# Row gathers without a bounds check, and VectorE operands read from PSUM, in a three-layer graph convolution

## What is computed

```python
deg = segment_sum(ones, dst)
norm = rsqrt(deg)[src] * rsqrt(deg)[dst]
def conv(h, W, b):
    xw = h @ W
    return segment_sum(xw[src] * norm[:, None], dst) + b
h = conv(conv(conv(x, W1, b1), W2, b2), W3, b3)
out = layernorm(x + h)          # over the 512 features, eps 1e-5
```

## Time and profile before

| | before |
|---|---|
| median of 3 runs | 3510.13 us (3508.68 to 3517.03) |
| profiled execution, its own time | 3509.13 us |
| its span in the trace | 3507.1 us |
| TensorE granted clock over the span | 0.963 |
| TensorE busy | 2637.4 us (75%) |
| GpSimd busy | 2574.0 us (73%) |
| VectorE busy | 1133.2 us (32%) |
| ScalarE busy | 126.9 us (4%) |

### The profile page before, as it was taken

One profiled execution on the slowest core, in us unless ns is written; L12 is line 12 of the kernel. 1 busy time (PEld: TensorE's weight loads), 2 busy tenths in 40 slices (PEclk: granted clock), 3 DMA queues, 4 the chain that ended last, 5 costly groups with the idle time before them and its releaser, 6 DMA issues.

```text
span 3507.1 us, 23852 instructions
## 1 busy us (share of the span) xinstructions
PE 2637.4 (75%) x6574; PEld 1095.7 (31%) x6574; DVE 1133.2 (32%) x2036; ACT 126.9 (4%) x222; POOL 2574.0 (73%) x2511
## 2 busy tenths in 40 slices
PE   7788888888888867777777777766777777777776
PEld 5233333333333322222222222222222222222222
DVE  7222222222222222222222222232434443443334
ACT  1000000000000000000000000000000000000000
POOL 0677777777777657777777777767777777777775
PEclk9999999999999989999999999998999999999998
DMA  8677777777777657777777777766777777777776
GB/s 292 200 211 208 209 207 207 207 204 207 210 207 206 194 154 212 209 209 210 210 208 206 209 208 206 207 193 194 220 216 222 220 219 220 219 223 218 221 213 180
DMA packets 243792, 736.23 MB, mean 210 GB/s; under 512 B 43286, under 2 KB 44946, under 8 KB 243664
## 3 DMA queue, kind: packets, MB, share of 16 engines
q0 software_dynamic: 199440, 653.68, 65.3%
q1 hardware_dynamic: 44224, 81.08, 6.3%
HBM read 683.39 MB, written 51.20 MB: 209 GB/s over the span
## 4 chain that ended last, share of the span: by engine, by line
POOL 48%; issue 14%; POOLq 1%; PE 1%; DMA 1%; DVE 0%; ACT 0%; DVEq 0%
POOL ring L386 48%; POOLq L386 1%; PE ps L549 1%; DMA y_dram<-acc 0%; DMA ring<-y_dram,src_idx 0%; PE ps L602 0%; DVE acc L879 0%; ACT acc L683 0%; DVEq L876 0%; DVE h_sb L901 0%; DVE ln L907 0%; DVE h_sb L905 0%; POOLq L77 0%; DVE row_sb L887 0%; DVE h_sb L887 0%
## 5 line engine op out<-in xcount | busy, mean ns | idle before, releaser
L386 POOL DMA_INDIRECT ring<-y_dram,src_idx x2493 | 2571.1, 1031 | 910.6 <-issue 758.9
L549 PE MATMUL ps<-ring,onehot 128*128 128x512 f32 x4986 | 2371.7, 622 | 829.3 <-DMA ring<-y_dram,src_idx 757.2
L549 PEld LDWEIGHTS ps<-ring,onehot 128*128 128x128 f32 x4986 | 938.4, 197 | 2226.8 <-issue 1792.8
L879 DVE SCALAR_TENSOR_TENSOR acc<-ps,mask,acc 128x512 f32 x624 | 439.8, 747 | 1291.5 <-PE ps L549 1171.5
L861 DVE TENSOR_TENSOR onehot<-place_iota,lo_f 128x512 f32<-128x512 f32 x624 | 428.8, 688 | 879.5 <-PE ps L549 879.5
L575 PE MATMUL ps<-w,w_sb 128*128 128x512 f32 x376 | 169.0, 592 | 0.0
L683 ACT ACTIVATE acc<-h_sb,dinv 128x512 f32<-128x512 f32 x96 | 69.3, 721 | 1488.8 <-DVE h_sb L887 1488.8
L575 PEld LDWEIGHTS ps<-w,w_sb 128*128 128x128 f32 x376 | 71.4, 190 | 89.9 <-issue 89.9
L887 DVE SCALAR_TENSOR_TENSOR h_sb<-ps,dinv,bias 128x512 f32<-128x512 f32 x48 | 36.0, 751 | 135.2 <-PE ps L575 128.9
L679 ACT ACTIVATE w_sb<-ps 128x512 f32<-128x512 f32 x47 | 28.1, 597 | 667.2 <-PE ps L559 667.2
L687 ACT ACTIVATE ln<-ln 128x1 f32<-128x1 f32 x49 | 9.9, 203 | 1123.2 <-DVE ln L913 1123.2
(11 more groups left out here) (105 smaller groups left out, 164.3 us busy)
## 6 DMA issues: line engine op xcount, KB each, us to landing
ring<-y_dram,src_idx POOLq DMA_INDIRECT x2493, 3.8
y_dram<-acc SPq DMA_DIRECT2D x96, 256.0 KB
acc<-in_x_dram SPq DMA_DIRECT2D x1, 12288.0 KB
y_dram<-acc SPq DMA_DIRECT2D x12, 1024.0 KB
w_sb<-in_x_dram SPq DMA_DIRECT2D x48, 256.0 KB, 4.7
out_dram<-row_sb SPq DMA_DIRECT2D x48, 256.0 KB
w_sb<-in_L_gnn_W_dram SPq DMA_DIRECT2D x1, 1024.0 KB
w<-in_L_gnn_W_dram SPq DMA_DIRECT2D x1, 1024.0 KB
```

The lines of the kernel that those rows point to most:

```text
L386: pool.indirect_dma_start(ring[:, s, :], None, y_dram[layer], bass.IndirectOffsetOnAxis(ap=rows, axis=0), bounds_check=N - 1, oob_is_err=F ...
L549: mm = pe.matmul(ps[:, g % BANKS, :], onehot[:, r, k, :], ring[:, r * CPQ + k, :], start=(opens and k == 0), stop=(closes and k == chunks ...
L879: dve.scalar_tensor_tensor(out=rows, in0=ps[:, g % BANKS, :], scalar=mask[:, part, own:own + 1], in1=rows, op0=ALU.mult, op1=ALU.add).then ...
```

## The change

The indirect DMA is issued without `bounds_check` and `oob_is_err`. ScalarE copies three kinds of operand from SBUF into PSUM, and VectorE reads them there:

- `place_iota` once in the prelude, into 128 columns of bank 7 (`iota_ps`), read by `stage_places`;
- the bias of layer 1, and later that of layer 2, into bank 5, at the start of each of these layers (`spread_bias`);
- the x rows of each tile of layer 2 but the last two into bank 4 (`spread_x`), after their load and after the x step of the tile before.

In `norm_rows` the first instruction now adds the bias and the second adds x. SP's queue now waits for the x copy (`x_spread`) before it loads the next x rows. Since bank 7 is taken, the last two tiles of layer 0 are turned into banks 4 and 6 in place of 6 and 7.

```diff
-        LAST_TURN_BANK, LAST_PRODUCT_BANK = 6, 2
+        LAST_TURN_BANKS, LAST_PRODUCT_BANK = (4, 6), 2
+        X_BANK, BIAS_BANK, IOTA_BANK = 4, 5, 7
+        iota_ps = ps[:, IOTA_BANK, 2 * P:3 * P]
...
             def load_and_finish(t):
                 if not is_static(t, 0):
-                    sp.wait_ge(ln_step, LN_STEPS * t + (1 - LN_STEPS))
+                    sp.wait_ge(x_spread, t)
...
                 pool.indirect_dma_start(ring[:, s, :], None, y_dram[layer],
-                                        bass.IndirectOffsetOnAxis(ap=rows, axis=0),
-                                        bounds_check=N - 1, oob_is_err=False).then_inc(done, 16)
+                                        bass.IndirectOffsetOnAxis(ap=rows, axis=0)).then_inc(done, 16)
...
-                        mm = pe.transpose(ps[:, LAST_TURN_BANK + j, k * P:(k + 1) * P], rows[:, k * P:(k + 1) * P], ident[:, :])
+                        mm = pe.transpose(ps[:, LAST_TURN_BANKS[j], k * P:(k + 1) * P], rows[:, k * P:(k + 1) * P], ident[:, :])
...
         def _(act):
+            act.wait_ge(consts_ready, CONSTS)
+            act.copy(iota_ps, place_iota[:, :]).then_inc(iota_spread, 1)
             act.wait_ge(edges_turned, 1)
...
+            def spread_bias(layer):
+                if layer > 0:
+                    act.copy(ps[:, BIAS_BANK, :], bias[:, layer, :]).then_inc(bias_spread, 1)
+
+            def spread_x(t):
+                act.wait_ge(x_loaded, 16 * t + 16)
+                if not is_static(t, 0):
+                    act.wait_ge(ln_step, LN_STEPS * t + (2 - LN_STEPS))
+                act.copy(ps[:, X_BANK, :], x_sb).then_inc(x_spread, 1)
...
             def fast_tile(layer, t):
...
                 else:
+                    spread_x(t)
                     std(t)
...
                 for layer in range(LAYERS):
+                    spread_bias(layer)
                     for t in range(LOOP_TILES):
                         fast_tile(layer, t)
...
-                dve.tensor_tensor(onehot[:, n % RING_QUADS, :, :], place_iota[:, :].unsqueeze(1).broadcast_to([P, CPQ, P]),
+                dve.tensor_tensor(onehot[:, n % RING_QUADS, :, :], iota_ps.unsqueeze(1).broadcast_to([P, CPQ, P]),
...
-                                         scalar=dinv[:, bass.ds(t, 1)], in1=bias[:, layer, :],
+                                         scalar=dinv[:, bass.ds(t, 1)], in1=bias[:, 0, :] if layer == 0 else ps[:, BIAS_BANK, :],
...
+                dve.scalar_tensor_tensor(out=row, in0=tile_of(t), scalar=dinv[:, bass.ds(t, 1)], in1=ps[:, BIAS_BANK, :],
+                                         op0=ALU.mult, op1=ALU.add).then_inc(ln_step, 1)
                 if last is None:
-                    dve.wait_ge(x_loaded, 16 * t + 16)
+                    dve.wait_ge(x_spread, t + 1)
...
-                dve.scalar_tensor_tensor(out=row, in0=tile_of(t), scalar=dinv[:, bass.ds(t, 1)],
-                                         in1=x_sb if last is None else last_x[last],
-                                         op0=ALU.mult, op1=ALU.add).then_inc(ln_step, 1)
                 dve.wait_ge(ln_step, done + 1)
-                dve.tensor_tensor(row, row, bias[:, LAYERS - 1, :], ALU.add).then_inc(ln_step, 1)
+                dve.tensor_tensor(row, row, ps[:, X_BANK, :] if last is None else last_x[last], ALU.add).then_inc(ln_step, 1)
...
                     dve.wait_ge(y_ready, TILES * layer)
+                    dve.wait_ge(bias_spread, layer)
...
+                dve.wait_ge(iota_spread, 1)
                 for n in range(EARLY_QUADS):
```

More of the change, by code:

```diff
@@ L178, in gcn_three_layers_resnorm @@
         ORDER_BANK, TURN_BANK, PRODUCT_BANK, DEG_BANK = 4, 4, 5, 7
-        LAST_TURN_BANK, LAST_PRODUCT_BANK = 6, 2
+        LAST_TURN_BANKS, LAST_PRODUCT_BANK = (4, 6), 2
+        X_BANK, BIAS_BANK, IOTA_BANK = 4, 5, 7
         GROUP_BANK = 4
+        iota_ps = ps[:, IOTA_BANK, 2 * P:3 * P]
         turned = ps[:, :, :].rearrange("p b n -> p (b n)")
         consts_ready = sem("consts_ready")
+        iota_spread = sem("iota_spread")
+        bias_spread = sem("bias_spread")
+        x_spread = sem("x_spread")
         pads_ready = sem("pads_ready")
@@ L710, in last_tiles @@
                         act.wait_ge(tile_turned, LOOP_TILES + k + 1)
-                        act.activation(last_turned[k], ps[:, LAST_TURN_BANK + k, :], ACT.Copy).then_inc(turn_copied, 1)
+                        act.activation(last_turned[k], ps[:, LAST_TURN_BANKS[k], :], ACT.Copy).then_inc(turn_copied, 1)
                 for k in range(2):
```

## The result

The changed kernel takes 3293.45 us (3293.05 to 3295.0, 4 runs), the kernel before 3510.9 us beside it. The ratio is 0.9379, with a 95% interval of 0.9363 to 0.9395: 217 us less, where 87 us less were forecast. The time lies in the range; the gain is two and a half times the forecast one.

A forecast was written before the change was run, and what follows sets the result against it. GpSimd's chain of 2493 gathers was taken to bound the kernel. From the median 3510.1 us, 83.1 us for moved operands and 3.6 us for the check came off, giving 3423.4 us, range 3282 to 3450.

The forecast's parts named there:

- The bound: GpSimd's chain sets the span: first gather at 106.0, gathers 2571.1, idle between them 808.3, tail 21.7, together 3507.1 us.
- Part 1: Iota, bias and x read from PSUM: gathers no longer held up by VectorE instructions with two SBUF tensors, -83.1 us.
- Part 2: Gathers without the bounds check: taken as one more column of a GpSimd instruction, 1.45 ns each, -3.6 us in all.
- The serial bound: Check inside the gather walking over the 128 rows one after the other at 1.45 ns: 185 ns each, 461 us.
- The first rival: The check inside each gather costs more, between 5 and 98 ns: 3415 down to 3183 us, 2966 if serial; chance 0.30.
- The MOVE: The check's instruction in GpSimd's queue, 0.03 us in the gap between gathers: free, the gap stays 0.30 us.
- Parts 3 to 6: VectorE's PSUM operands, ScalarE's copies, layer 2's x chain and the exchanged banks: nothing added to the forecast time.
- part 3: VectorE instructions with a PSUM operand: some 6 ns slower each, 5 us on an engine that waits, nothing in the tail.
- part 5: Layer 2's x load, ScalarE copy, then VectorE: 11.5 us left, 3.6 us for the one early tile; cost 0.
- PSUM without effect: Rival: one-hots hold up the gather wherever their iota lies, so only the check's 3.6 us are gained: 3506.5 us; chance 0.05.
- a late x: Rival: layer 2's x copy misses its 11.5 us and VectorE's additions stall 0.5 us in 47 tiles: 3447 us; chance 0.03.
- a dearer unchecked gather: Rival: the gather without the check takes another, dearer path in its code; at 98 ns more, 3671 us; chance 0.05.

## Why the prediction came out as it did

**The bound: right.** The span was read as a sum on GpSimd, and after the change the same four terms sum to it again.

**Part 1, the moved operands: right in mechanism and size.** Forecast -83.1 us. With the check kept, the gathers went from 2571.1 to 2490.2 us, -80.9; the missing 2.2 us are in 28 gathers that were held up under the last scaling of a tile, 3.3 us together (see the last section). This third cause the prediction didn't have: it said that no gather would be above some 1010 ns, and the longest are 1199 ns there and 1116 ns in the changed kernel. Nor did it have that the operands are worth more without the check: 92.7 us (2450.5 to 2357.8), because more gathers then began under a one-hot. Of the rule in the Trainium skill ("SBUF — State Buffer", Who interferes with whom), the part on two SBUF inputs agrees with all four kernels whose one-hots read SBUF, by 0.21 to 0.24 us for each gather that begins under one, and with the four that read PSUM, by less than 0.002 us. From the same section the prediction took the inference that such an instruction would not hold up a DMA. For these indirect DMAs the measurement differs, and decides. Whether what waits is the gather's read of its index list or something else in it, no run shows.

**Part 2, the bounds check: the step that failed.** Of the three bounds I took "one more column of a GpSimd instruction", 1.45 ns and 3.6 us in all; it measured 52 ns and 129.6 us. The reasoning that led there was "the index list has one column, so it is nearest to the first row". That compares the shape of the operand; what the chip showed is a price that hardly depends on the rows, 42 ns at 32 and at 64 of them. The nearer row was the one that I put at the other end, the shortest whole instruction with 98 ns, almost all of it fixed. The serial bound (185 ns) is out as well, and with it my remark in the rivals that 7.8 ns a row speaks for work row by row: 128 rows against 32 are 81 ns. The first rival, "the check is dear", is the case that happened, at 0.30; its span of 3183 to 3415 us holds the time, and the range reached to it.

**The MOVE: right.** The gap was 0.30 us with and without it. Reading the end of the queue, where MOVEs had run out, gave the answer ahead of time.

**Parts 3 to 6: nothing on the path, as forecast, with a wrong sign in part 3 and a thin margin in part 5.** VectorE's instructions with a PSUM operand are not slower but 3 to 8 ns faster (685 against 688, 737 against 745), so the sign of part 3 was wrong and its size nothing. Among x copies the early tile came closest: its copy began at 3261.52 us, and the x addition at 3262.98 us, right behind the step before it:

```profile
3257.04 0.43 SPq L331 DMA_DIRECT2D w_sb<-in_x_dram  x1
3261.52 0.59 ACT L699 COPY ps<-w_sb 128x512 f32<-128x512 f32 x1 [5.68 <-DMA w_sb<-in_x_dram]
3262.13 0.75 DVE L917 SCALAR_TENSOR_TENSOR h_sb<-acc,dinv,ps 128x512 f32<-128x512 f32 x1 [2.67 <-PE ps L553]
3262.98 0.69 DVE L924 TENSOR_TENSOR h_sb<-h_sb,ps 128x512 f32<-128x512 f32 x1
```

That leaves 0.9 us. The prediction had 3.6 us from the rows of before, and one instruction (some 0.8 us) on top. The margin shrank because the tile's first step now came 5.1 us after the load was issued (3257.04 to 3262.13), against 8.9 us in the earlier trace rows. The copy ended 0.02 us ahead of that first step, so with the x addition first it would just have been in time as well; no run tried that order. Every other tile had over 9 us.

**The other rivals.** PSUM without effect, a late x and a dearer unchecked gather are each out by the rows above.

## What to carry to other kernels

Where one short instruction repeated thousands of times sets the pace, take its minimum, median and maximum first. The spread tells what others do to it (here VectorE instructions with two SBUF tensors), and can be priced from the trace; an option of the instruction itself hides in the minimum, which no trace without that option can price. Give such an option a wide share of the range, or measure it alone. Here the gather was mostly fixed cost (865 of 946 ns at a quarter of the rows) and so was the option; that another option behaves so is a guess. And a gain on the pacing engine shows only where it does set the pace: the kernel with the check as an error was 1.5% faster than the kernel before on one chip, and not faster (3787.79 against 3783.91 us) on the one where the engines waited for something else and TensorE's mean clock was 0.878.

## What the runs showed that was not expected

**A gather of 32 rows costs 865 ns, one of 128 rows 946.** From 32 to 128, rows are nearly free; what counts is the number of instructions.

**The scaling of a finished tile and a gather hold each other up, in either order.** In the kernel before, 38 of its 49 instances began 0.49 to 0.50 us after a gather began and took 0.72 to 0.74 us; the others took 0.55. Start plus lengthening comes to 0.68 us into the gather. Without the check it comes to 0.65 us, from five starts between 0.44 and 0.62 us (iota from SBUF) and 33 between 0.54 and 0.55 us (check taken off). So the gather holds the scaling up to that moment, and not to its own end at 0.95 or 1.00 us. A gather and the lengthened scaling that began under it, then one of the short ones, from the timeline of the kernel before:

```profile
3448.42 1.00 POOL L386 DMA_INDIRECT ring<-y_dram,src_idx  x1 [0.30 <-issue]
...
3448.92 0.73 DVE L919 TENSOR_SCALAR row_sb<-h_sb,ln 128x512 f32<-128x512 f32 x1
```

```profile
3469.98 0.55 DVE L919 TENSOR_SCALAR row_sb<-h_sb,ln 128x512 f32<-128x512 f32 x1
```

That they began at the same point of a gather I put down to the two instructions of the same tile with two SBUF tensors (bias and x additions): they hold up the gather ahead, and so bring the two engines into step. No run tests this by itself, but the runs fit it. With bias and x in SBUF the starts fall together without the check too (33 of 49 within 0.01 us when only the check is off; 32 of 49 in two clusters hardly wider with the iota in PSUM). With every operand in PSUM they don't: with the check put back most are spread from 0.71 to 1.09 us, and in the changed kernel they are spread over the gather, and the group's mean fell from 690 to 551 ns (with it the 33.1 us of VectorE's time to 26.4). In the other order the gather waits, as in the timeline of the changed kernel:

```profile
3056.50 0.55 DVE L938 TENSOR_SCALAR row_sb<-h_sb,ln 128x512 f32<-128x512 f32 x1
```

```profile
3056.76 1.12 POOL L391 DMA_INDIRECT ring<-y_dram,src_idx  x1 [0.30 <-issue]
```

This instruction has one SBUF input; the Trainium skill (the same section) names VectorE's two-port modes as a second cause. The trace fits this, 512 columns in 0.55 us against 0.69 for the two-tensor form, but it doesn't record the mode. The prediction gave the rule without this exception. Gathers held up by this instruction are most of what is left of the excess: 0.6 us in the changed kernel, 3.3 us with the check put back.
